# One more convolution chunk of a feed-forward layer on the vector engine, one fewer on GpSimd

## The chip, the cores and the metric

The kernel runs on all 8 cores of one Trainium2 chip. Each core computes one of the 8 sequences of the batch alone; nothing is exchanged between the cores. The metric is the device time in microseconds (us) of the slowest core. The engines are called as in the profile: PE (TensorE), DVE (the vector engine), ACT (the scalar engine), POOL (GpSimd) and SP (the queue that issues most transfers).

## The reference

One macaron layer on x of shape (8, 8192, 1024): half a feed-forward block, a retention block without softmax, half a feed-forward block again, with a layer norm ahead of each.

```python
def ffn(x, w1, conv_w, conv_b, w2):        # hidden size 4096
    h = bit_linear(x, w1)                  # x quantised by row to 8 bits, w1 to -1, 0, 1
    h = depthwise_conv1d(h)                # 3 taps along the sequence, one filter per channel
    h = silu(h + conv_b)
    return bit_linear(h, w2)               # h quantised by its row maximum

x = x + 0.5 * ffn(layernorm(x))
x = x + attn(layernorm(x))
x = x + 0.5 * ffn(layernorm(x))
```

The convolution, per channel c and position s, is `w[c,0]*h[s-1] + w[c,1]*h[s] + w[c,2]*h[s+1]`.

## The kernel before

The program has four parts, one after the other, with a barrier of all engines between them: the weights are quantised, then passA (the first feed-forward layer), passB (retention), passC (the second feed-forward layer). passA and passC are the same function, `ffn_phase`, on other tensors.

A pass takes the 8192 positions in 16 blocks of 512. Channels lie on the 128 partitions: the 4096 hidden channels are 32 chunks of 128. A block's first product (W1, `emit_w1_mm`, L530) fills a buffer `hb` of 32 chunks by 512 positions, which ACT copies out of PSUM (L542). The rest is done in two windows of 256 positions for each block.

- **First window** (`emit_w1_convA`): POOL convolves 8 of the 32 chunks, DVE 24 (L577, L581, L585), while PE runs W1 for the next block. Halfway, the output of the window before is written out by DVE.
- **Second window** (`emit_conv_silu(bw, 1)`): the constant `NCONV_B` divides the chunks. DVE takes chunks 0 to `NCONV_B - 1`, each in three instructions (L652, L657, L662). POOL takes the others, each in five (L488, L494, L498, L502, L506). With 20 there are 20 chunks on DVE and 12 on POOL: 60 instructions on each engine. Meanwhile PE runs the second product (W2, L780) of the first window.

ACT applies silu to every chunk in place, in an order written out by hand: POOL's chunk 20 (L641), DVE's chunk 0 (L666), POOL's chunk 21, DVE's chunk 1, and so on to POOL's chunk 31 and DVE's chunk 11, and then DVE's chunks 12 to 19. An engine takes its instructions in the order in which they are written, so a silu that waits for POOL holds all that follow it:

```python
for cc in range(NCC):                      # NCC = 32
    if cc < NCC - NCONV_B:
        # ACT: silu of POOL's chunk NCONV_B + cc, waits for POOL (L641)
    if cc >= NCONV_B:
        continue
    # DVE: three convolution instructions of chunk cc (L652, L657, L662)
    # ACT: silu of chunk cc, waits for DVE (L666)
```

Behind its 20 chunks, DVE writes out the first window (`emit_yevac`, L806 and L811, four instructions, which wait for W2). Then comes `emit_trees_scale_quant`: a tree of maxima and minima over the 32 chunks (it begins at L682 and waits for ACT's last silu), transposes on PE (L699) and row maxima on DVE (L704 and on), a scale, and then in eight groups a product on POOL (L748) and two casts on DVE (L753, L757). The first casted group releases the second window's W2 on PE (L780). Behind that W2, PE runs W1 for the next block, and behind W1 the transposes (L699) of the next first window. SP issues the weight loads (two ahead), the stores of the output and the loads of the residual.

Of the kernel before, what the change touches and what calls it, by code (L numbers as in the profile page):

```python
# [29 lines left out]
ENGS = ("tensor", "vector", "scalar", "gpsimd", "sync")  # L30
NCONV_V = 22
NCONV_A = 24
NCONV_B = 20


class Ctr:
# [49 lines left out]
def build_program():  # L86
# [246 lines left out]
    def ffn_phase(src_h, dst_h, m_t, r_t, mr_t, out_sum, out_sq, name):  # L333
        pfx = name + "_"
        rec = Rec(chain={"vector": cv, "scalar": cs, "gpsimd": cg})
        with contextlib.ExitStack() as ps:
# [291 lines left out]
            def emit_conv_silu(bw, wdx):  # L628
                hbuf = hb[bw % 2]
                base = 1 + 256 * wdx  # L630
                for cc in range(NCONV_B, NCC):
                    fw = []
                    if cc == NCONV_B:
                        fw = [(cs, hev_s.get(bw, 0)),
                              (cv, halo_r.get(bw, 0))]
                    emit_conv_cc_pool(cc, hbuf, base, fw, defer_silu=True)
                for cc in range(NCC):
                    if cc < NCC - NCONV_B:
                        pcc_ = NCONV_B + cc
                        rec.emit("scalar",  # L640
# [3 lines left out]
                                 waits=[(cg, pool_cc_n[pcc_])])  # L644
                    if cc >= NCONV_B:
                        continue
# [629 lines left out]
```

How the kernel before makes its waits and increments, by code:

```python
            def run(e):  # L69
                for w, fn, inch, by in ops:
                    for h, v in w:
                        e.wait_ge(h, v)
                    ins = fn(e) if fn is not None else None
                    if inch is not None:
                        if ins is None:
                            ins = e.nop()
                        ins.then_inc(inch, by)
```

## Time and profile before

| | us |
|---|---|
| median of the 2 runs shown | 10379.87 |
| the two runs | 10322.69 and 10437.04 |
| the profiled execution, its time | 10041.3 |
| its span, slowest core (core 5) | 10039.8 |
| spans of its eight cores | 9962.4 to 10039.8 |

All rows are of the profiled execution, on core 5. Its time is 1.5 us more than its span, and 339 us less than the median of the runs. In the page's 40 slices, passA fills slices 4 to 17 and passC slices 26 to 40; passB and the weight preparation are not touched by the change. A block of passC takes about 230 us.

### The profile page before, as it was taken

What the parts mean: (1) busy time and instruction counts of PE and PEld (TensorE: products, weight loads), DVE (VectorE), ACT (ScalarE), POOL (GpSimd) and SP (SyncE); (2) the same over time, 40 slices, a digit from 0 to 9 for tenths busy, and PEclk for the clock granted to TensorE, in tenths of its full rate; (3) what the DMA queues carried; (4) which work ended last, traced back from release to release, by engine and by line L of the source; (5) the groups of instructions that cost most, each with busy time, mean ns of one, the idle gap of its engine ahead of it and who ended that gap; (6) DMA issues with size and microseconds to landing.
All of it is one profiled execution on the core that took longest, in us unless ns stands there. A gap on an engine that the chain in (4) does not pass through costs nothing. (4 is left out here: it accounts for less than half of the span.)

```text
span 10039.8 us, 106003 instructions; the slowest of 8 cores (9962.4 to 10039.8 us)
## 1 busy us (share of the span) xinstructions
PE 5673.1 (57%) x25288; PEld 2498.0 (25%) x25288; DVE 6390.0 (64%) x9475; ACT 2497.1 (25%) x4235; POOL 3401.6 (34%) x3852
## 2 busy tenths in 40 slices
PE   0055555565555556367778886655556555555554
PEld 0022222222222222123333333222222222222221
DVE  6647777777767777723323233577777767777777
ACT  0332322233232222211111111322223222222221
POOL 0224444444444445400000000344444444444444
PEclk9987778878777778678888888777788877778777
DMA  7734444444444434231100111343444444444433
GB/s 241 241 115 137 145 130 138 139 139 138 143 133 130 128 124 143 92 88 34 34 34 34 38 38 61 109 143 126 139 142 142 147 136 128 130 128 147 132 118 113
DMA packets 515042, 1204.59 MB, mean 120 GB/s; under 512 B 25744, under 2 KB 26000, under 8 KB 514448
## 3 DMA queue, kind: packets, MB, share of 16 engines
q1 hardware_dynamic: 498960, 1141.19, 36.0%
q0 software_dynamic: 15488, 56.63, 1.9%
q8 instruction: 232, 3.80, 0.2%
q14 instruction: 362, 2.97, 0.1%
HBM read 1086.57 MB, written 117.44 MB: 120 GB/s over the span
## 5 line engine op out<-in xcount | busy, mean ns | idle before, releaser
L780 PE MATMUL passA_pw<-passA_w2r,passA_nb 128*128 128x512 bf16 x4096 | 1063.9, 423 | 421.6 <-DMA passA_w2r<-w2q 294.8
L780 PE MATMUL passC_pw<-passC_w2r,passC_nb 128*128 128x512 bf16 x4096 | 1043.3, 417 | 405.7 <-DMA passC_w2r<-w2q 279.1
L748 POOL TENSOR_TENSOR passA_vqb<-passA_zb,passA_s2b 128x1024 f32<-128x1024 bf16 x256 | 631.1, 2465 | 1610.2 <-DVE passA_s2b L735 1368.4
L748 POOL TENSOR_TENSOR passC_vqb<-passC_zb,passC_s2b 128x1024 f32<-128x1024 bf16 x256 | 631.2, 2466 | 1591.5 <-DVE passC_s2b L735 1349.2
L488 POOL TENSOR_TENSOR passC_zb<-passC_hb,cwb_s 128x256 bf16<-128x256 bf16 x320 | 200.9, 628 | 2247.4 <-ACT passC_hb L542 2017.3
L530 PE MATMUL passA_pw<-passA_m1f,passA_w1r 128*128 128x512 bf16 x4096 | 911.3, 383 | 46.9 <-DMA passA_w1r<-w1q 34.7
L530 PE MATMUL passC_pw<-passC_m1f,passC_w1r 128*128 128x512 bf16 x4096 | 907.9, 382 | 45.5 <-DMA passC_w1r<-w1q 34.7
L1028 PE MATMUL b_pq<-b_xn2f,b_wq 128*128 128x512 bf16 x3072 | 694.8, 384 | 31.5 <-DMA b_wq<-wqkvT 31.5
L780 PEld LDWEIGHTS passA_pw<-passA_w2r,passA_nb 128*128 128x128 bf16 x4096 | 426.9, 107 | 1057.3 <-issue 702.8
L780 PEld LDWEIGHTS passC_pw<-passC_w2r,passC_nb 128*128 128x128 bf16 x4096 | 420.4, 105 | 1027.2 <-issue 661.4
L753 DVE CAST passA_niqb<-passA_vqb 128x1024 int32<-128x1024 f32 x256 | 504.6, 1971 | 104.6 <-POOL passA_vqb L748 80.8
L753 DVE CAST passC_niqb<-passC_vqb 128x1024 int32<-128x1024 f32 x256 | 500.9, 1957 | 104.6 <-POOL passC_vqb L748 80.8
L465 PE MATMUL passA_ptr<-identb_s,passA_m1tm 128*128 128x128 bf16 x512 | 64.7, 306 | 886.2 <-DVE passA_m1tm L457 886.2
L1151 DVE SCALAR_TENSOR_TENSOR b_y2st<-b_pro,evk_s,b_yl 128x512 f32<-128x512 f32 x128 | 96.1, 751 | 719.8 <-PE b_pro L1135 718.5
L530 PEld LDWEIGHTS passA_pw<-passA_m1f,passA_w1r 128*128 128x128 bf16 x4096 | 397.7, 98 | 557.8 <-issue 105.7
L530 PEld LDWEIGHTS passC_pw<-passC_m1f,passC_w1r 128*128 128x128 bf16 x4096 | 397.7, 98 | 552.9 <-issue 97.5
L542 ACT CAST passA_hb<-passA_pw 128x512 bf16<-128x512 f32 x512 | 301.5, 589 | 640.4 <-PE passA_pw L530 623.7
L542 ACT CAST passC_hb<-passC_pw 128x512 bf16<-128x512 f32 x512 | 301.5, 589 | 618.4 <-PE passC_pw L530 602.5
L465 PE MATMUL passC_ptr<-identb_s,passC_m1tm 128*128 128x128 bf16 x512 | 64.7, 306 | 650.2 <-DVE passC_m1tm L457 650.2
L1028 PEld LDWEIGHTS b_pq<-b_xn2f,b_wq 128*128 128x128 bf16 x3072 | 304.0, 99 | 406.4 <-issue 53.8
L1035 ACT ACTIVATE b_qf<-b_pq,bqkv_s 128x512 bf16<-128x512 f32 x128 | 88.0, 687 | 1053.0 <-PE b_pq L1028 1053.0
L488 POOL TENSOR_TENSOR passA_zb<-passA_hb,cwb_s 128x256 bf16<-128x256 bf16 x320 | 201.1, 629 | 344.9 <-DVE passA_hb L621 182.8
(178 smaller groups left out, 10409.3 us busy)
## 6 DMA issues: line engine op xcount, KB each, us to landing
passA_w2r<-w2q SPq DMA_DIRECT2D x256, 1024.0 KB, 6.4
passC_w2r<-w2q SPq DMA_DIRECT2D x256, 1024.0 KB, 6.1
passA_w1r<-w1q SPq DMA_DIRECT2D x128, 1024.0 KB, 5.7
passC_w1r<-w1q SPq DMA_DIRECT2D x128, 1024.0 KB, 5.6
p_w<-w1s SPq DMA_DIRECT2D x64, 512.0 KB, 5.5
p_w<-w2s SPq DMA_DIRECT2D x64, 512.0 KB, 5.3
p_x<-x POOLq DMA_DIRECT2D x64, 512.0 KB, 5.5
passA_xln<-x SPq DMA_DIRECT2D x64, 512.0 KB, 3.6
```

Of the source, the lines that this page charges most:

```text
L465: lambda e, dc=dc, sx=m1tm[k % 2]: e.transpose(ptr[:, dc * 128:(dc + 1) * 128], sx[:, dc * 128:(dc + 1) * 128], identb[:]),
L488: e.tensor_tensor(zb[:, cc, :].unsqueeze(2), hbuf[:, cc, base - 1:base + 255].unsqueeze(2), w, OP.mult), waits=first_waits)
L530: e.matmul(bank[:], w1r[:, slot, dc, :], m1f[:, dc, mcol:mcol + 512], start=(dc == 0), stop=(dc == NDC - 1)),
L542: lambda e, cc=cc, hb_=hb[b % 2], bank=bank: e.copy(hb_[:, cc, 1:513], bank[:]),
L748: rec.emit("gpsimd", lambda e, g=g, hfq=hfq: e.tensor_tensor(vqb[:, hfq:hfq + 4, :], zb[:, 4 * g:4 * g + 4, :], s2b[:].unsqueeze(1).broadc ...
L753: rec.emit("vector", lambda e, hfq=hfq: e.tensor_copy(niqb[:], vqb[:, hfq:hfq + 4, :]), waits=[(cg, vq_done[g])])
L780: lambda e, cc=cc, ti=ti, hf=hf: e.matmul(pw2[2 * ti + hf][:], nbf[:, cc, ti * 128:(ti + 1) * 128], w2r[:, cc % 8, hf * 512:(hf + 1) * 512 ...
L1028: rec.emit("tensor", lambda e, tc=tc, oc=oc, dc=dc: e.matmul(pq[oc % 2][:], wq[dc][:, oc * 128:(oc + 1) * 128], xn2f[tc % 2][:, dc, :], st ...
L1035: rec.emit("scalar", lambda e, oc=oc, d=dsts: e.activation(d[:, oc % 8, :], pq[oc % 2][:], AF.Identity, bias=bqkv[:, oc:oc + 1]), waits=[( ...
L1151: e.scalar_tensor_tensor(y2st[ysl][:, hf * 512:(hf + 1) * 512], pro[hf][:], evk[:, it:it + 1], ylr[k % 8][:, hf * 512:(hf + 1) * 512], OP. ...
```

## The change

The constant `NCONV_B` goes from 20 to 21:

```diff
-NCONV_B = 20
+NCONV_B = 21
```

It is used only in `emit_conv_silu`. In each second window chunk 20 moves from POOL to DVE: POOL issues 55 instructions instead of 60, DVE 63 instead of 60, and ACT 32 silus as before, 11 of them behind POOL and 21 behind DVE. In ACT's order POOL's last chunk now stands ahead of DVE's chunk 10, so DVE's chunks 10 to 20 come behind it. On POOL the chunks begin with 21. No transfer, buffer or wait is added. There are 16 second windows in each of the two passes, 32 in all.

## Rows read from the trace of the kernel before

**Rows 1.** The page: its first line, and busy time of each engine.

```profile
span 10039.8 us, 106003 instructions; the slowest of 8 cores (9962.4 to 10039.8 us)
PE 5673.1 (57%) x25288; PEld 2498.0 (25%) x25288; DVE 6390.0 (64%) x9475; ACT 2497.1 (25%) x4235; POOL 3401.6 (34%) x3852
```

**Rows 2.** The waits: who waited for whom: us in total, times, longest us.

```profile
DVE passC_nb L682 <- ACT passC_zb L666: 56.3, 16, 4.2
DVE passA_nb L682 <- ACT passA_zb L666: 51.8, 16, 3.7
...
ACT passC_zb L641 <- POOL passC_zb L506: 614.9, 192, 51.6
...
DVE passC_ystg L806 <- PE passC_pw L780: 21.8, 1, 21.8
...
DVE passC_tq L704 <- PE passC_ptr L699: 228.9, 32, 16.5
```

**Rows 3.** Timeline, second window of one passC block: start us, us, engine, line.

```profile
7637.12 0.29 DVE L652 TENSOR_SCALAR passC_zb<-passC_hb,cwq_s 128x256 bf16<-128x256 bf16 x1
7637.22 0.66 POOL L488 TENSOR_TENSOR passC_zb<-passC_hb,cwb_s 128x256 bf16<-128x256 bf16 x1 [12.69 <-DVE passC_hb L621]
...
7679.20 0.67 POOL L506 TENSOR_TENSOR passC_zb<-passC_zb,passC_cvt 128x256 bf16<-128x256 bf16 x1
7679.24 0.91 DVE L657 SCALAR_TENSOR_TENSOR passC_zb<-passC_hb,cwq_s,passC_zb 128x256 bf16<-128x256 bf16 x1
7679.68 1.89 PE L780 MATMUL passC_pw<-passC_w2r,passC_nb 128*128 128x512 bf16 x8
7680.02 0.51 ACT L641 ACTIVATE passC_zb<-passC_zb,cbv_s 128x256 bf16<-128x256 bf16 x1 [2.78 <-POOL passC_zb L506]
7680.25 0.65 DVE L662 SCALAR_TENSOR_TENSOR passC_zb<-passC_hb,cwq_s,passC_zb 128x256 bf16<-128x256 bf16 x1
7680.62 0.51 ACT L666 ACTIVATE passC_zb<-passC_zb,cbv_s 128x256 bf16<-128x256 bf16 x1
...
7682.57 0.65 DVE L662 SCALAR_TENSOR_TENSOR passC_zb<-passC_hb,cwq_s,passC_zb 128x256 bf16<-128x256 bf16 x1
7683.08 0.67 POOL L506 TENSOR_TENSOR passC_zb<-passC_zb,passC_cvt 128x256 bf16<-128x256 bf16 x1
7683.32 0.75 DVE L806 SCALAR_TENSOR_TENSOR passC_ystg<-passC_pw,passC_evsc,passC_xres 128x512 f32<-128x512 f32 x1
7683.90 0.51 ACT L641 ACTIVATE passC_zb<-passC_zb,cbv_s 128x256 bf16<-128x256 bf16 x1 [2.77 <-POOL passC_zb L506]
7684.50 5.31 ACT L666 ACTIVATE passC_zb<-passC_zb,cbv_s 128x256 bf16<-128x256 bf16 x9
...
7685.89 0.75 DVE L811 SCALAR_TENSOR_TENSOR passC_ystg<-passC_pw,passC_evsc,passC_xres 128x512 f32<-128x512 f32 x1
...
7690.05 2.29 DVE L682 TENSOR_TENSOR passC_nb<-passC_zb 128x4096 bf16<-128x4096 bf16 x1 [3.41 <-ACT passC_zb L666]
```

**Rows 4.** Timeline, first window of a passC block, where POOL's chunks end.

```profile
7538.38 0.67 POOL L506 TENSOR_TENSOR passC_zb<-passC_zb,passC_cvt 128x256 bf16<-128x256 bf16 x1
7538.63 0.51 DVE L577 TENSOR_SCALAR passC_zb<-passC_hb,cwq_s 128x256 bf16<-128x256 bf16 x1
7539.24 0.48 DVE L581 SCALAR_TENSOR_TENSOR passC_zb<-passC_hb,cwq_s,passC_zb 128x256 bf16<-128x256 bf16 x1
...
7539.83 0.48 DVE L585 SCALAR_TENSOR_TENSOR passC_zb<-passC_hb,cwq_s,passC_zb 128x256 bf16<-128x256 bf16 x1
...
7540.42 0.29 DVE L577 TENSOR_SCALAR passC_zb<-passC_hb,cwq_s 128x256 bf16<-128x256 bf16 x1
...
7541.99 0.29 DVE L577 TENSOR_SCALAR passC_zb<-passC_hb,cwq_s 128x256 bf16<-128x256 bf16 x1
```

**Rows 5.** Timeline, behind the maxima: vector engine at L704, TensorE at L780.

```profile
7586.09 0.29 DVE L704 TENSOR_REDUCE passC_tq<-passC_ptr 128x1 f32<-128x128 bf16 x1 [12.71 <-PE passC_ptr L699]
...
7716.21 4.00 PE L780 MATMUL passC_pw<-passC_w2r,passC_nb 128*128 128x512 bf16 x9 [7.02 <-DVE passC_nb L757]
```

## The prediction, made before the changed kernel was run

> **What bounds the kernel now.** I first read the page's busy times [rows 1]: no engine is busy for more than 64% of the span (DVE), so no total decides, and a change is worth what it is worth in the place where it stands. DVE is the engine to look at, but the question is what it waits for there.
>
> Next the waits [rows 2]. The tree of maxima (L682) opens the work behind a window's convolution. In the second windows it waits for ACT's last silu (L666), 16 times in each pass: 56.3 and 51.8 us, 108 us in all, 3.4 us each time. So when DVE is ready, ACT is not. ACT in its turn waits for POOL at L641, 614.9 us in passC.
>
> Then the timeline of one second window [rows 3], to see the order of the ends. DVE and POOL begin together, at 7637.12 and 7637.22. DVE's last convolution instruction ends at 7682.57 + 0.65 = 7683.22, POOL's at 7683.08 + 0.67 = 7683.75. Both need 46 us for 60 instructions: about 0.777 us for one of each. After this ACT takes the silu of POOL's last chunk at 7683.90, and then nine silus of DVE chunks, whose data had long been there, from 7684.50 for 5.31 us, to 7689.81. DVE meanwhile writes out the first window, from 7683.32 to 7685.89 + 0.75 = 7686.64, and idles 3.41 us, until 7690.05. What sets the tree's start is thus POOL's last chunk plus ten silus that queue behind it.
>
> Last, whether a tree that starts earlier is worth its whole gain [rows 2, 5]. Behind the tree, PE's W2 waits for DVE's casts: PE had idled 7.02 us at 7716.21. W1 follows W2 on PE, and the next block's maxima (L704) wait for PE: 12.71 us at 7586.09, 228.9 us over passC's 32. The way from the tree goes through PE's products, with some 13 us to spare on DVE. Neither product changes, so all of it moves with the tree. I take a gain here as a gain of the span, for each of the 32 windows.
>
> **POOL.** Five instructions go. Chunk 11 ended at 7679.20 + 0.67 = 7679.87 [rows 3], and it becomes POOL's last: POOL's end moves forward by 7683.75 − 7679.87 = 3.88 us. POOL then has nothing to do until the scale is there.
>
> **DVE.** Three instructions come. While both engines work, an instruction of the one goes with one of the other, and DVE's take longer: 0.91 us at 7679.24 [rows 3]. At the end of POOL's share in a first window one sees what happens when POOL stops [rows 4]: POOL's last instruction ends at 7539.05, and from 7539.24 on DVE's take 0.48, 0.48 and 0.29 us, and a chunk lasts 7541.99 − 7540.42 = 1.57 us, not three times 0.777 = 2.33. The forms are the same, so 1.57 is my price. With POOL done at 7679.87, DVE finishes chunk 18 (the 19th) with an instruction at 7680.25 that takes 0.48 instead of 0.65, to 7680.73; two more chunks end at 7683.87. That is 0.65 us later than before. The output takes 3.42 us as before (7686.64 − 7683.22), to 7687.29, and the next instruction could start at about 7687.4. W2, for which the output waits, ended at 7681.57 [rows 3]; over passC that output waited for W2 once only [rows 2], so W2 stays covered.
>
> The bounds of this price: below, the 1.57 us chunk; above, 0.777 an instruction if DVE does not speed up. The 63 instructions would then end 2.33 us later than the 60 did, at 7685.55, the output at 7688.97, and the tree would start at about 7689.1: a gain of only 1.0 us. I take the lower price because the rows 4 show the same three instructions at the moment when POOL stops.
>
> **ACT.** The silus are 32 as before, 0.60 us apart: nine take 5.31. The silu of POOL's eleventh chunk stands at 7680.02 in the trace and is now POOL's last. At 7680.62 comes DVE's chunk 10, and now ten more follow, chunks 11 to 20, without waiting for POOL again: the last ends at 7680.62 + 10 × 0.60 + 0.51 = 7687.13. The last one's data are there at 7683.87, in time. From ACT's end to the tree took 0.24 us before (7690.05 − 7689.81), so by ACT the tree could start at 7687.37.
>
> **The sum.** DVE (7687.4) and ACT (7687.4) arrive together; the tree starts 7690.05 − 7687.4 = 2.65 us earlier, and what would be late next is both at once, so a further chunk would bring nothing. Thirty-two windows give 32 × 2.65 = 85 us. Its largest value, if DVE's three instructions were hidden and ACT's tail did not grow, is POOL's 3.88 us: 124 us. Its smallest is the 1.0 us above: 32 us. The added and removed instructions cause no transfer; SP's store of the output moves by 0.65 us and nothing waits for it within the window.
>
> **The rule of the port.** The rows show that DVE's 0.48 us instruction takes up to 0.91 beside POOL [rows 3, 4], and that a pair takes 0.777 us. If the two engines never overlapped, a pair would take about 0.63 + 0.42 = 1.05 us (the means of POOL's 0.61 and 0.67, and of DVE's 0.29, 0.48 and 0.48), and 60 pairs 63 us, where 46 are measured. They overlap in part. The Trainium skill, "SBUF — State Buffer", section "Who interferes with whom", says that the pair of ports that these two engines share is locked for a whole instruction and that the other fully blocks. By that rule the sum would go by port time, and it is the fourth rival below; the measured pair speaks against its strict form.
>
> **The rivals.**
>
> *DVE does not speed up.* Its added instructions keep the pace of 0.777 us, or W2 ends late and holds the output. The gain is 1.0 us a window, 32 us in all. Against it: the rows 4. Chance 0.14, with all mixed values between 1.0 and 2.3 us.
>
> *The gain is lost behind the tree,* in PE's wait for weights or in the transposes: 0 us. For it: PE's products take most of a block. Against it: PE waits for DVE at 7716.21 [rows 5]. Chance 0.08.
>
> *The longer DVE queue decides: slower.* The tree starts where DVE's end puts it, later by 0.65 us (21 us over 32) up to 2.33 us (75 us). This holds only from the point where the added chunk eats the whole 3.41 us of idle time ahead of L682 [rows 3]; 2.33 does not reach it. Chance 0.04.
>
> *Ports in strict turn.* Both engines' ends are then set by the sum of instruction times, in which 3.17 us of POOL's (three at 0.61, two at 0.67) are replaced by 1.25 of DVE's: 1.92 us a window, 61 us in all. Chance 0.06. The Trainium skill's page named above states the rule behind it.
>
> *More than forecast,* up to 124 us: 0.04. The forecast itself: 0.64.
>
> **How the numbers follow.** On the profiled execution's own scale the forecast is 10041.3 − 85 = 9956 us, and between 9940 and 9980 for the likeliest case alone. The two runs shown lie 281 and 396 us above the profiled one, and their median 339 us; the rows are of the profiled execution, and they do not say why. Taking the 85 us off the median gives 10379.87 − 85 = 10295 us, which I predict; the likeliest case alone spans 10280 to 10320 there. In ratio, it is 0.8% to 0.9% less. The terms are known far better than the level: two executions of one program differ by more than this change is worth. So the range has to hold both levels: from 9935 (the profiled level less some 106 us, between forecast and the upper bound) to 10400 (the median plus 21 us for the slower case).
>
> A measurement of this kernel can tell about 2% from no change, which is 208 us, or 6.5 us for each window. No rival reaches it: the whole end of POOL moves by 3.88. So within 2% gets 0.93; faster 0.05 and slower 0.02 are what is left for a mechanism that I do not see.
>
> **What would show it right or wrong.** In the changed kernel's timeline: POOL's last L506 about 42.7 us after the window's first L652 (46.6 before); DVE's last L662 at 46.8; the last instructions of DVE at 0.48 us; twelve silus on ACT with no wait from the eleventh POOL chunk on; DVE's idle time ahead of L682 down from 3.4 us to about 0.1 (the waits row L682 <- ACT L666 close to nothing); the tree 50.3 us after the window's start, 52.9 before. The wait of L704 for PE stays near 13 us, and a block takes 2.65 us less. If the tree starts earlier and blocks are no shorter, the step to the span was wrong; if DVE's last chunks take 2.33 us, the price was.

## The result, and the profile after

The ratio of the times after to before is 0.9917, with a 95% interval of 0.9883 to 0.9951; the medians of all runs are 10187.09 us (28 runs) and 10220.03 us (26). The forecast on the profiled execution's own scale, 9956 of 10041.3 us, is a ratio of 0.9915.

In some executions of either kernel half of the cores, or all of them, take longer (in the profile after cores 0 to 3, mostly in passB, which the change does not touch: 2518 us on core 0 and 2294 on core 4, from passA's last second window to passC's first one), which mixes two levels into the medians, so the ratio is taken from undisturbed executions and I read core 4.

The waits of DVE after, on core 4 (us in total, times, longest us):

```profile
DVE passC_tq L704 <- PE passC_ptr L699: 235.3, 32, 17.5
...
DVE passC_ystg L806 <- PE passC_pw L780: 17.7, 1, 17.7
DVE passC_nb L682 <- ACT passC_zb L666: 2.7, 5, 0.7
DVE passA_nb L682 <- ACT passA_zb L666: 2.2, 3, 0.9
```

The wait of the tree (L682) for ACT's last silu was 56.3 and 51.8 us [rows 2] and is 2.7 and 2.2. The wait of L704 for PE stays: 235.3 where 228.9 stood.

One second window of passC after, timeline of core 4 (start us, us, engine, line):

```profile
7066.85 0.28 DVE L652 TENSOR_SCALAR passC_zb<-passC_hb,cwq_s 128x256 bf16<-128x256 bf16 x1
...
7108.94 0.67 POOL L506 TENSOR_TENSOR passC_zb<-passC_zb,passC_cvt 128x256 bf16<-128x256 bf16 x1
7108.98 0.91 DVE L657 SCALAR_TENSOR_TENSOR passC_zb<-passC_hb,cwq_s,passC_zb 128x256 bf16<-128x256 bf16 x1
7109.75 0.51 ACT L641 ACTIVATE passC_zb<-passC_zb,cbv_s 128x256 bf16<-128x256 bf16 x1 [2.77 <-POOL passC_zb L506]
7109.99 0.48 DVE L662 SCALAR_TENSOR_TENSOR passC_zb<-passC_hb,cwq_s,passC_zb 128x256 bf16<-128x256 bf16 x1
7110.35 6.51 ACT L666 ACTIVATE passC_zb<-passC_zb,cbv_s 128x256 bf16<-128x256 bf16 x11
7110.58 0.29 DVE L652 TENSOR_SCALAR passC_zb<-passC_hb,cwq_s 128x256 bf16<-128x256 bf16 x1
...
7112.15 0.29 DVE L652 TENSOR_SCALAR passC_zb<-passC_hb,cwq_s 128x256 bf16<-128x256 bf16 x1
...
7113.13 0.48 DVE L662 SCALAR_TENSOR_TENSOR passC_zb<-passC_hb,cwq_s,passC_zb 128x256 bf16<-128x256 bf16 x1
7113.72 0.75 DVE L806 SCALAR_TENSOR_TENSOR passC_ystg<-passC_pw,passC_evsc,passC_xres 128x512 f32<-128x512 f32 x1
...
7116.28 0.75 DVE L811 SCALAR_TENSOR_TENSOR passC_ystg<-passC_pw,passC_evsc,passC_xres 128x512 f32<-128x512 f32 x1
...
7117.14 2.29 DVE L682 TENSOR_TENSOR passC_nb<-passC_zb 128x4096 bf16<-128x4096 bf16 x1
```

Read it against rows 3, counted from the window's first L652:

| us from the first L652 | before [rows 3] | forecast | after |
|---|---|---|---|
| POOL's last chunk ends | 46.63 | 42.75 | 42.76 |
| ACT takes its silu | 46.78 | 42.90 | 42.90 |
| ACT's last silu ends | 52.69 | 50.01 | 50.01 |
| DVE's last convolution instruction ends | 46.10 | 46.75 | 46.76 |
| DVE's output ends | 49.52 | 50.17 | 50.18 |
| the tree starts (L682) | 52.93 | 50.28 | 50.29 |

Eleven silus now stand behind POOL's last, in one row of 6.51 us, and they end at 7116.86. DVE's last instructions take 0.48 us and its chunks 1.57 us (7110.58 to 7112.15). The tree follows the output with no idle time.

It is much the same in all windows of a core (50.3 to 51.3 us on core 4, 52.7 to 53.7 before on core 5), and the rest of a block has not moved, apart from PE's two products. The table gives means over 28 blocks of a core (the last two of each pass have no W1 behind them); where one figure stands, the eight cores differ by at most 0.12 us.

| part of a block, us | before | after |
|---|---|---|
| second window, first L652 to the tree L682 | 53.1 | 50.5 |
| tree to the first scaled group (L748) | 19.73 | 19.75 |
| to the first matmul of W2 (L780) | 6.21 | 6.22 |
| W2 of the second window | 40.1 to 41.6 | 39.5 to 42.1 |
| W1 of the next block | 58.1 to 60.7 | 57.9 to 60.1 |
| transposes L699 to the first scaled group | 8.36 | 8.38 |
| to the next second window | 42.53 | 42.57 |

Over all 32 windows the first part takes 1699.6 us before (core 5) and 1617.7 after (core 4): 82 us less. 82 of 10041 us are 0.8%, which is the gain in the ratio. The two profiles by themselves lie further apart (core 4: 10032.3 us before, 9878.7 after), mostly because PE's two products came out shorter on this core, 98.8 us a block for 101.2; over the eight cores their sum is 99.3 to 101.2 us before and 98.8 to 101.0 after, so nothing here shows that the change made them shorter.

### The profile page after: what moved, and what is told of

Its sections match the earlier page's. It is cut to its first block and busy times, and to the rows that moved or that the text cites. A ratio compares the mean times of both kernels' runs of the same rounds, so it can differ in the third digit from the quotient of the medians.

```text
span 10175.8 us, 105875 instructions; the slowest of 8 cores (9860.4 to 10175.8 us)
## 1 busy us (share of the span) xinstructions
PE 5960.6 (59%) x25288; PEld 2570.4 (25%) x25288; DVE 6402.5 (63%) x9571; ACT 2497.2 (25%) x4235; POOL 3304.0 (32%) x3692
## 5 line engine op out<-in xcount | busy, mean ns | idle before, releaser
L780 PE MATMUL passA_pw<-passA_w2r,passA_nb 128*128 128x512 bf16 x4096 | 1066.1, 424 | 381.8 <-DMA passA_w2r<-w2q 254.6
L780 PE MATMUL passC_pw<-passC_w2r,passC_nb 128*128 128x512 bf16 x4096 | 1039.6, 417 | 393.8 <-DMA passC_w2r<-w2q 266.8
L748 POOL TENSOR_TENSOR passA_vqb<-passA_zb,passA_s2b 128x1024 f32<-128x1024 bf16 x256 | 631.4, 2466 | 1634.8 <-DVE passA_s2b L735 1391.3
L748 POOL TENSOR_TENSOR passC_vqb<-passC_zb,passC_s2b 128x1024 f32<-128x1024 bf16 x256 | 631.4, 2466 | 1608.4 <-DVE passC_s2b L735 1366.9
L530 PE MATMUL passA_pw<-passA_m1f,passA_w1r 128*128 128x512 bf16 x4096 | 956.8, 397 | 20.1 <-DMA passA_w1r<-w1q 9.6
L1028 PE MATMUL b_pq<-b_xn2f,b_wq 128*128 128x512 bf16 x3072 | 818.0, 432 | 21.6 <-DMA b_wq<-wqkvT 21.6
L780 PEld LDWEIGHTS passA_pw<-passA_w2r,passA_nb 128*128 128x128 bf16 x4096 | 425.9, 107 | 1020.1 <-issue 703.3
L780 PEld LDWEIGHTS passC_pw<-passC_w2r,passC_nb 128*128 128x128 bf16 x4096 | 421.7, 106 | 1010.3 <-issue 644.4
L753 DVE CAST passA_niqb<-passA_vqb 128x1024 int32<-128x1024 f32 x256 | 503.3, 1966 | 103.9 <-POOL passA_vqb L748 80.2
L753 DVE CAST passC_niqb<-passC_vqb 128x1024 int32<-128x1024 f32 x256 | 501.6, 1959 | 104.3 <-POOL passC_vqb L748 80.2
L1028 PEld LDWEIGHTS b_pq<-b_xn2f,b_wq 128*128 128x128 bf16 x3072 | 332.6, 108 | 490.0 <-issue 450.1
```

What stands on the lines that cost most here:

```text
L530: e.matmul(bank[:], w1r[:, slot, dc, :], m1f[:, dc, mcol:mcol + 512], start=(dc == 0), stop=(dc == NDC - 1)),
L748: rec.emit("gpsimd", lambda e, g=g, hfq=hfq: e.tensor_tensor(vqb[:, hfq:hfq + 4, :], zb[:, 4 * g:4 * g + 4, :], s2b[:].unsqueeze(1).broadc ...
L753: rec.emit("vector", lambda e, hfq=hfq: e.tensor_copy(niqb[:], vqb[:, hfq:hfq + 4, :]), waits=[(cg, vq_done[g])])
L780: lambda e, cc=cc, ti=ti, hf=hf: e.matmul(pw2[2 * ti + hf][:], nbf[:, cc, ti * 128:(ti + 1) * 128], w2r[:, cc % 8, hf * 512:(hf + 1) * 512 ...
L1028: rec.emit("tensor", lambda e, tc=tc, oc=oc, dc=dc: e.matmul(pq[oc % 2][:], wq[dc][:, oc * 128:(oc + 1) * 128], xn2f[tc % 2][:, dc, :], st ...
```

## The experiments

The theory: the silus that queue on ACT behind POOL's last chunk set the tree's start, and with 21 chunks DVE's own end, with the output behind it, has caught up with them. The first rival: POOL's share is what counts, and less work on POOL with less contention is the gain. The second: DVE's longer queue decides. A window is counted from its first L652 to the tree; figures are medians over the eight cores of means over 32 windows. For three kernels (22 chunks, and 20 and 21 with the new order) the runs gave no ratio; for them the windows speak.

**19 chunks on DVE.**

```diff
-NCONV_B = 20
+NCONV_B = 19
```

> The constant goes the other way, 19 chunks on the vector engine and 13 on GpSimd. A window is measured from its first L652 to its tree (L682): a mean of 53.1 us before, 50.5 with 21. Theory (the silus queued behind GpSimd's last chunk set the tree): GpSimd's 65 instructions at 0.777 us end at about 50.5 us, its last silu and seven more follow, the tree starts at about 55.7 us, 2.6 us later than before: 32 x 2.6 = 83 us slower, and as much by the blocks. Rival (the tree is set by the longer queue of the vector engine): the window gets shorter, since that engine has 57 instructions: about 0.7 us a window, 21 us faster.

Measured: a window takes 55.9 us, DVE idles 8.55 us ahead of the tree, and the ratio to the kernel before is 1.005 (0.9995 to 1.0104), an interval that holds both no change and the expected 83 us. The timeline of core 1, a window that begins at 7378.00:

```profile
7417.30 0.61 POOL L488 TENSOR_TENSOR passC_zb<-passC_hb,cwb_s 128x256 bf16<-128x256 bf16 x1
...
7421.19 0.61 POOL L488 TENSOR_TENSOR passC_zb<-passC_hb,cwb_s 128x256 bf16<-128x256 bf16 x1
...
7422.18 0.75 DVE L806 SCALAR_TENSOR_TENSOR passC_ystg<-passC_pw,passC_evsc,passC_xres 128x512 f32<-128x512 f32 x1
...
7424.75 0.75 DVE L811 SCALAR_TENSOR_TENSOR passC_ystg<-passC_pw,passC_evsc,passC_xres 128x512 f32<-128x512 f32 x1
7425.07 0.61 POOL L488 TENSOR_TENSOR passC_zb<-passC_hb,cwb_s 128x256 bf16<-128x256 bf16 x1
...
7428.15 0.67 POOL L506 TENSOR_TENSOR passC_zb<-passC_zb,passC_cvt 128x256 bf16<-128x256 bf16 x1
7428.96 0.51 ACT L641 ACTIVATE passC_zb<-passC_zb,cbv_s 128x256 bf16<-128x256 bf16 x1 [2.78 <-POOL passC_zb L506]
7429.56 4.11 ACT L666 ACTIVATE passC_zb<-passC_zb,cbv_s 128x256 bf16<-128x256 bf16 x7
7433.91 2.29 DVE L682 TENSOR_TENSOR passC_nb<-passC_zb 128x4096 bf16<-128x4096 bf16 x1 [8.42 <-ACT passC_zb L666]
```

POOL ends at 7428.82, its last silu and seven more follow (4.11 us), and the tree waits 8.42 us for them, although DVE was done with everything at 7425.50. So DVE's queue does not set the tree here, and the second rival falls. The window is 2.8 us longer where 2.6 was expected.

**22 chunks on DVE.**

```diff
-NCONV_B = 20
+NCONV_B = 22
```

> One more chunk moves, 22 on the vector engine and 10 on GpSimd. Theory: from 21 on the vector engine's own end and the output that it writes (3.4 us) set the tree; its convolution ends at about 47.5 us instead of 46.8, the tree starts 51.0 to 51.2 us after the window's start: 0.65 us a window more than with 21 (21 us slower than that kernel), 2.0 us less than before (64 us faster than before). Scalar engine's idle time before the tree: none that decides; the tree waits for nothing. Rival (the gain comes from GpSimd's share alone, the less work it has, the less both engines stand in each other's way): another 2.6 us a window, 47.9 us, 165 us faster than before.

Measured: a window takes 50.7 us, DVE idles 0.12 us ahead of the tree (between two instructions that wait for nothing). The gain ends at 21, as the theory has it, and the first rival, which expected 47.9 us, is out. But the expected 0.65 us over the kernel with 21 came out as 0.16. The price of a chunk was mis-sized: five pairs at 0.777 us go (3.89) and eight instructions alone come, at 1.57 / 3 = 0.523 us (4.19), a difference of 0.30; about that much, 0.33, stands between this kernel (50.68) and the one with 21 chunks and the new order below (50.35), and in both DVE alone sets the tree.

**20 chunks, ACT's order by completion.** No chunk moves; a silu of POOL's chunk is put behind that silu of DVE's beside which it is done:

```diff
-for cc in range(NCC):
-    if cc < NCC - NCONV_B:
-        # ACT: silu of POOL's chunk NCONV_B + cc
+nxt = NCONV_B
+for cc in range(NCONV_B):
+    while nxt < NCC and 5 * (nxt - NCONV_B + 1) <= 3 * cc:
+        # ACT: silu of POOL's chunk nxt
+        nxt += 1
     # DVE: convolution of chunk cc;  ACT: its silu
+while nxt < NCC:
+    # ACT: silu of POOL's chunk nxt
+    nxt += 1
```

> No chunk moves (20 and 12, as before). Only the scalar engine's order changes: a silu of GpSimd's chunk is put where that chunk is done, so that no silu of the vector engine's chunks stands behind the last of GpSimd's. Theory: the tail of nine silus goes; by the scalar engine the tree could start at about 47.5 us, so the vector engine's output (done at 49.5 us) sets it: about 49.7 us, 3.3 us a window less than before, 106 us faster than before, 21 us faster than with 21 chunks. Rival (the gain of the change comes from less work for GpSimd and less contention): the work is the same, so the window stays at 53.1 us and the time is that of before.

Measured: a window takes 49.8 us (49.7 expected), 3.3 us less than before with the same work on every engine. The profiled execution takes 9894.8 us, 146 less than the one of before; 3.3 × 32 = 106 of these are the windows, the rest, 40, is 1.3 us a block, which is of the size by which PE's products differ between the cores of one execution. Timeline of core 0 (L668 and L639 are the silus of DVE's and POOL's chunks here, L811 and L816 the output, L687 the tree):

```profile
7343.22 0.65 DVE L664 SCALAR_TENSOR_TENSOR passC_zb<-passC_hb,cwq_s,passC_zb 128x256 bf16<-128x256 bf16 x1
7343.73 0.67 POOL L506 TENSOR_TENSOR passC_zb<-passC_zb,passC_cvt 128x256 bf16<-128x256 bf16 x1
7343.97 0.75 DVE L811 SCALAR_TENSOR_TENSOR passC_ystg<-passC_pw,passC_evsc,passC_xres 128x512 f32<-128x512 f32 x1
7344.02 0.51 ACT L668 ACTIVATE passC_zb<-passC_zb,cbv_s 128x256 bf16<-128x256 bf16 x1 [1.22 <-DVE passC_zb L664]
7344.62 0.51 ACT L639 ACTIVATE passC_zb<-passC_zb,cbv_s 128x256 bf16<-128x256 bf16 x1
...
7346.53 0.75 DVE L816 SCALAR_TENSOR_TENSOR passC_ystg<-passC_pw,passC_evsc,passC_xres 128x512 f32<-128x512 f32 x1
7347.39 2.29 DVE L687 TENSOR_TENSOR passC_nb<-passC_zb 128x4096 bf16<-128x4096 bf16 x1
```

POOL's last instruction ends at 7344.40, its silu is the last one and ends at 7345.13, and the tree starts at 7347.39 right behind the output. This separates theory and first rival: the tail alone is worth more than the whole change, and less work on POOL is not needed for it.

**21 chunks, the same order.**

```diff
-NCONV_B = 20
+NCONV_B = 21
```

with the order of the kernel above.

> 21 chunks on the vector engine and the scalar engine's order by completion as well. Theory: with 21 chunks the vector engine's convolution and output (50.2 us) and the scalar engine's last silu (50.0 us) arrive together, so taking the scalar engine's tail away gains nothing: the tree at 50.3 to 50.5 us as with 21 alone, the scalar engine done at about 47.4 us, and the vector engine without idle time ahead of the tree. 85 us faster than before, and 0 (within 10 us) against 21 alone. Rival (the scalar engine alone still sets the tree): about 47.7 us, another 85 us.

Measured: 50.35 us a window and 0.10 us of idle time ahead of the tree. Against 21 chunks alone (50.52) the order brings 0.17 us, so DVE's end and its output set the tree, as forecast.

**21 chunks, the output behind the tree.** The first window's output (`emit_yevac`) is split; its first two instructions stand ahead of L735, the scale, its last two behind it. Only the call is shown here:

```diff
-emit_yevac(bw, 0, pw0)
-bf1 = emit_trees_scale_quant(bw, 1, s_silu1)
+bf1 = emit_trees_scale_quant(bw, 1, s_silu1,
+          out_cb=lambda ti: emit_yevac(bw, 0, pw0, (ti,)))
```

> 21 chunks on the vector engine, and the output of the first window (L806, L811) is no longer written ahead of the tree but behind it, two instructions ahead of the scale (L735) and two behind it, where the vector engine waits for TensorE and GpSimd. Theory: the scalar engine's last silu (50.0 us) now sets the tree alone, so the tree stays at 50.3 us; the vector engine idles about 3.3 us ahead of it, as before the change; behind the tree at most 0.3 us are added. Against 21 alone: 0 to 10 us slower, 75 to 85 us faster than before. Rival (only the vector engine sets the tree with 21 chunks): the tree at 47.0 us, 105 us faster than 21 alone.

Measured: 50.50 us a window and 3.67 us of idle time ahead of the tree: ACT alone holds it at the same place. The waits of DVE on core 0 (L683 is the tree here):

```profile
DVE passC_nb L683 <- ACT passC_zb L666: 59.9, 16, 4.4
DVE passA_nb L683 <- ACT passA_zb L666: 58.6, 16, 4.4
```

The part behind the tree, to the first scaled group, takes 20.05 us instead of 19.75. The ratio to the kernel before is 0.9896 (0.9819 to 0.9973). So each of the two ends alone keeps the tree at 50.3 to 50.5 us.

**21 chunks, both.** Order by completion and output behind the tree, the two edits above together.

> Both at once: the scalar engine's order by completion and the output behind the tree, 21 chunks. Theory: the two ends that arrived together at 50.3 us are both taken away; what is left is the vector engine's last chunk (46.8 us), its silu and the step to the tree, about 47.7 us: 2.7 us a window less than with 21 alone, less 0.2 to 0.3 us behind the tree, 75 to 85 us faster than 21 alone and 160 to 170 us faster than before, while either of the two by itself brings nothing. Rival (behind the tree another wait takes the gain, TensorE's weights or the second product): the tree at 47.7 us but blocks no shorter than with 21 alone.

Measured: 47.77 us a window (47.7 expected), the part behind the tree 20.05 us, the ratio 0.984 (0.9752 to 0.9928). Timeline of core 0 (L668 the silu of DVE's chunks, L688 the tree):

```profile
7343.92 0.67 POOL L506 TENSOR_TENSOR passC_zb<-passC_zb,passC_cvt 128x256 bf16<-128x256 bf16 x1
...
7348.11 0.48 DVE L664 SCALAR_TENSOR_TENSOR passC_zb<-passC_hb,cwq_s,passC_zb 128x256 bf16<-128x256 bf16 x1
7348.75 0.51 ACT L668 ACTIVATE passC_zb<-passC_zb,cbv_s 128x256 bf16<-128x256 bf16 x1 [1.06 <-DVE passC_zb L664]
7349.49 2.29 DVE L688 TENSOR_TENSOR passC_nb<-passC_zb 128x4096 bf16<-128x4096 bf16 x1 [0.90 <-ACT passC_zb L668]
...
7367.05 0.75 DVE L816 SCALAR_TENSOR_TENSOR passC_ystg<-passC_pw,passC_evsc,passC_xres 128x512 f32<-128x512 f32 x1
7367.09 1.19 PE L737 MATMUL passC_paux<-passC_srow,ones_r 1*128 1x256 f32 x2 [0.73 <-DVE passC_srow L734]
```

What is left ahead of the tree is DVE's last instruction, one silu and the step between engines. The output's first instruction at 7367.05 lies beside PE's matmul at 7367.09, for which DVE used to wait (L735 for L731: 48.4 us over the 32 windows of passC before). Neither edit brought anything alone, and both bring 2.7 us a window: two ends that arrive together have to be moved together.

**The same once more.** In that run W1 took 60.2 to 63.1 us a block, where before it took 58.1 to 60.7.

> The kernel with 21 chunks, the order by completion and the output behind the tree, once more, since its first products (W1) took 60.2 to 61.0 us on its undisturbed cores where 58 to 60 were usual, about 1.3 us a block of a gain of 2.5. If this is a cost of the edit, W1 takes above 60 us on all undisturbed cores again and the kernel is about 130 us faster than before. If it is the spread of executions (58.1 to 60.7 between the cores of the kernel before), it falls back to a mean of about 59 us, and the kernel is 160 to 170 us faster than before.

Measured: a ratio of 0.9817 (0.9752 to 0.9883), windows of 47.75 us, and W1 at 58.2 to 61.6 us, with a mean of 59.9 over the cores (59.5 before). So most of the longer W1 was the spread of executions; whether 0.4 us a block belong to the edit stays open.

**20 chunks, both.**

> 20 chunks as before the change, with the scalar engine's order by completion and the output behind the tree. Theory: with both tails gone the tree follows the last end of either engine's convolution: GpSimd's 60 instructions at its own pace (46.6 us), one silu, 47.5 to 47.8 us. That is the same as 21 chunks with both (47.77 us), so where a chunk is convolved makes no difference any more, although it made 2.6 us in the kernels with the old order. 160 us faster than before, within 10 us of 21 chunks with both. Rival (the chunk that moved is worth something by itself): 50.4 us, 2.6 us a window more than 21 with both.

Measured: 47.80 us a window and a ratio of 0.9853 (0.9765 to 0.9941). With the two tails gone, it makes no difference to the window whether chunk 20 is on POOL or on DVE (47.80 and 47.75), although with the old order it made 2.6 us.

**The same edit in the first windows.**

```diff
-NCONV_A = 24
+NCONV_A = 25
```

> The same edit at another place: one chunk of the first windows goes from GpSimd to the vector engine (25 and 7 instead of 24 and 8), the second windows as before (20 and 12). Theory: in the first windows the vector engine waits about 13 us for TensorE at L704 behind the tree, so neither a gain nor a loss of one or two us ahead of it reaches the end: the time of before, within 15 us, the wait at L704 longer or shorter by what the tree moves. Rival (less work for GpSimd gains wherever it is): about 2.6 us for each of 32 windows, 85 us faster.

Measured: the ratio is 0.9988 (0.9896 to 1.008), an interval too wide to exclude the rival's 85 us by itself. The parts of a block do: those outside PE's two products sum to 129.97 us on core 7, where they sum to 129.98 on core 7 before (53.15 + 19.75 + 6.22 + 8.36 + 42.49, and 53.12 + 19.73 + 6.21 + 8.39 + 42.53). PE's two products take 98.6 to 100.4 us a block on cores 4 to 7, and 99.3 to 101.2 on the eight cores before: a difference of about 1 us stays open there, not 2.6. The wait for PE behind the tree is still there, on core 4:

```profile
DVE passA_tq L704 <- PE passA_ptr L699: 211.8, 32, 15.9
DVE passC_tq L704 <- PE passC_ptr L699: 189.2, 32, 12.5
```

A chunk fewer on POOL is worth nothing where PE is waited for.

## Why the prediction came out as it did

**The place** was right: 108 us of waiting ahead of L682 in the second windows [rows 2] have gone to 4.9 us. **POOL's 3.88 us** was right to 0.01. **DVE's price** was the lower bound, 1.57 us a chunk, as rows 4 had it; its end came 0.66 us later, forecast 0.65. **ACT's eleven silus** end where they were put. **The step to the span** was right: no other part of a block changed by more than 0.1 us, apart from PE's products, which differ as much between the cores of one execution. The sum was 85 us, and 82 were measured in the windows: the mean window started its tree 2.56 us earlier on core 4 and not 2.65. In six of its 32 windows POOL's last chunk ends at 43.1 to 43.3 us instead of 42.8, and ACT's last silu then holds the tree a few tenths longer than the output does (idle time ahead of the tree 0.23 us in the mean, not 0.1).

**What failed is in "How the numbers follow"**, at two steps; the mechanism and its sum held. The first is the level: "Taking the 85 us off the median". The term 10379.87 is the median of two runs, and both lay high (10322.69 and 10437.04; of 26 runs the lowest is 10014.94 and the median 10220.03). The level was thus 160 us too high, about twice the effect, and the 10295 us that were predicted for the faster kernel are 75 us more than the median of these 26 runs of the kernel before, and 108 more than was measured after. The medians moved by 33 us; the ratio of 0.9917 is 83 us of some 10040. The second: "A measurement of this kernel can tell about 2% from no change", from which within 2% got 0.93 and faster 0.05. The time did come within 2%, but no row of the prediction shows the 2%: the interval is 0.34% to either side, so 0.8% is told apart from no change, and the kernel is faster, by what the sum had said. With 0.04 on the one rival that ends slower and 0.08 on the one that ends at nothing, the sum should have been put as faster.

**The rivals.** *DVE does not speed up*: it did, at once, 0.48 us at 7109.99. *Lost behind the tree*: the parts of a block say no. *The longer DVE queue decides*: with 21 it sets the tree together with ACT, and with 22 alone, but the tree still starts 2.4 us earlier than before. *Ports in strict turn*: a pair would have cost 1.05 us, and the kernel with 19 chunks shows why it costs 0.777: beside DVE's convolution POOL does not pay at all. In that kernel its chunks follow one another at 3.89 us beside DVE's convolution (7417.30 to 7421.19) and at 3.88 beside the output (7421.19 to 7425.07), and the last one, alone from 7425.50 on, takes 3.75 to its end, as a chunk does beside DVE in the kernel before: 7679.87 [rows 3] − 7676.12, its first instruction:

```profile
7676.12 0.61 POOL L488 TENSOR_TENSOR passC_zb<-passC_hb,cwb_s 128x256 bf16<-128x256 bf16 x1
```

The pace of a pair is POOL's own pace, and of the two only DVE is slowed. The pair of 0.777 us, which the prediction took to speak against strict turns, does not refute them (the last section has the rows); what failed in this rival is that both ends go by the sum of the recorded times.

"A further chunk would bring nothing" was right (50.7 with 22, 50.5 with 21). What the prediction did not look for was the cheaper edit: its own reading, that nine silus whose data are there stand behind one that waits, says that the order is to be changed, and that is worth 3.3 us a window with no chunk moved.

## What to carry to other kernels

Where two engines share a job and a third consumes it in a fixed order, look at how many finished pieces stand behind the last unfinished one: that tail is paid each time, and an order by completion removes it without moving any work. Before moving work, list the ends of all chains that meet at the next step; the gain stops at the second of them (here after one chunk), and two that arrive together must be shortened together. Give the chances on the scale of what many runs can tell, and take the level from more than two.

## What the runs showed of the hardware

- Beside POOL's bf16 products and sums, DVE's convolution instructions take 0.45 to 0.51, 0.85 to 0.91 and 0.65 to 0.71 us, alone 0.29, 0.48 and 0.48. POOL's pace does not change there: a chunk of five instructions takes 3.75 us from its first start to its last end beside DVE (7676.12 to 7679.87 in the kernel before) and without it (7425.07 to 7428.82 with 19 chunks).
- DVE's output, which reads one operand from PSUM and one from SBUF, and a scalar for each partition, takes 0.75 us beside POOL (7422.18 in the kernel with 19 chunks) and 0.75 alone (7113.72 after). The Trainium skill, "SBUF — State Buffer", section "Who interferes with whom", says that a DVE instruction with at most one SBUF input, outside the faster two-port modes, does not contend with GpSimd; the trace agrees.
- POOL can be slowed too, beside DVE's casts (L753, L757), which its first chunk meets at the start of the first windows (rows below): its instructions take 0.87 to 0.93 us there, 0.61 and 0.67 elsewhere, and the casts 0.91 to 0.97 where either takes 0.69 (L753 at 7484.97, L757 at 7500.87). Each starts some 0.4 us before the other's ends and is longer by that overlap less 0.14 us.
- Beside the convolution the same turns leave POOL as it is. Its instruction at 7511.98 starts 0.14 us before DVE's of 7511.22 ends, and takes 0.61; so do some 2000 others of that core. DVE's start further ahead of the end of POOL's and are longer by their overlap less 0.20 us (7511.22: POOL's of 7511.17 ends at 7511.84, an overlap of 0.62, and 0.90 stands for 0.48). The recorded times of two instructions thus overlap by 0.14 and 0.20 us at no cost, and the 1.05 us of the prediction counts these twice. By an estimate from these numbers, 1.05 − 0.14 − 0.20 = 0.71 us, a pair in turns fits in the 0.777 us that POOL takes for an instruction beside DVE's output as well (3.88 / 5).
- The Trainium skill, "SBUF — State Buffer", section "Who interferes with whom", says of DVE's two-port modes that whichever of the two issues first gets the shared ports for its whole instruction and that the other fully blocks. Up to the 0.14 and 0.20 us the traces agree, beside the casts and beside the convolution; no run here shows which mode an instruction was in.

Kernel before, core 5:

```profile
7507.05 0.88 POOL L488 TENSOR_TENSOR passC_zb<-passC_hb,cwb_s 128x256 bf16<-128x256 bf16 x1
7507.56 0.92 DVE L757 CAST passC_nb<-passC_niqb 128x1024 bf16<-128x1024 int32 x1
7508.06 0.87 POOL L494 TENSOR_TENSOR passC_cvt<-passC_hb,cwb_s 128x256 bf16<-128x256 bf16 x1
7508.57 0.91 DVE L753 CAST passC_niqb<-passC_vqb 128x1024 int32<-128x1024 f32 x1
...
7511.17 0.67 POOL L506 TENSOR_TENSOR passC_zb<-passC_zb,passC_cvt 128x256 bf16<-128x256 bf16 x1
7511.22 0.90 DVE L581 SCALAR_TENSOR_TENSOR passC_zb<-passC_hb,cwq_s,passC_zb 128x256 bf16<-128x256 bf16 x1
...
7511.98 0.61 POOL L488 TENSOR_TENSOR passC_zb<-passC_hb,cwb_s 128x256 bf16<-128x256 bf16 x1
```
